# State-space layer of a 12-layer kernel: the bounds of plus and minus ten on B times delta, on GpSimd instead of VectorE

## Chip, cores and metric

The kernel runs on one core of a Trainium2 chip, as one launch that computes all twelve layers. The metric is the device time of that launch in microseconds (us), lower is better. Each engine has its own in-order queue of instructions: TensorE (PE in the profile, its weight loads PEld), VectorE (DVE), ScalarE (ACT), GpSimd (POOL) and SyncE (SP), which only issues DMAs. Engines are ordered against each other by semaphores alone.

## What is computed

The input is x of 64 sequences of 32 tokens with 128 features, so 2048 tokens. Twelve layers follow one another, each `x = x + layer(layernorm(x))`. The change touches the second one, the state-space layer `_L0_attn_ref`, whose front part is this (S is 16 states per feature):

```python
delta = jax.nn.softplus(x @ W_delta + b_delta)
Bm, Cm = x @ W_B, x @ W_C
A = -jnp.exp(A_log)
def step(h, inp):
    x_t, d_t, B_t, C_t = inp
    bar_A = jnp.exp(jnp.minimum(d_t[..., None] * A, 10.0))
    bar_B = jnp.clip(d_t[..., None] * B_t[:, None, :], -10.0, 10.0)
    h = jnp.clip(bar_A * h + bar_B * x_t[..., None], -10000.0, 10000.0)
    y_t = jnp.sum(h * C_t[:, None, :], axis=-1) + x_t * D_param
    return h, y_t
```

Behind it every token goes through the two best of four gated experts (a router, SiLU of one product times another, a root mean square norm, a down projection), and the sum is normed again.

## The kernel before, in words

The class `L0Attn` keeps features on the 128 partitions and tokens along the free axis. The 2048 tokens are cut into four quarters of 512 tokens (16 sequences of 32). For each quarter there are 16 states, so the layer has 64 units of work that the code calls states j = 0 to 63, each a tile of 128 x 512 fp32 words. All tiles lie in one SBUF tensor, `arena`; `PS` is PSUM. The tile `Ur[j % 8]` is used in place through a state's whole life, a ring of eight:

- TensorE (line 1002) spreads row B of the state over the partitions into PSUM; VectorE multiplies it by delta into `Ur` (line 1324, event `a0_db`).
- VectorE bounds it to plus and minus ten with one two-operation `tensor_scalar` in place (line 1334, `a0_clipped`).
- GpSimd multiplies it by x in place (line 1189, `a0_u`).
- ScalarE made the decay `Ar` (line 1122, an exponential); VectorE runs the recurrence over the tokens with `tensor_tensor_scan` on `Ar` and `Ur` (line 1329, `a0_scanned`).
- TensorE spreads row C (line 1002 again); VectorE multiplies (line 1319, `a0_read`); TensorE adds the result into PSUM with an identity matrix (line 1046). After 16 states VectorE adds x times D (line 1313) and the quarter is done.

All engines walk the same numbered steps i, in program order, and the order of the work is written out by hand as offsets from i. In step i VectorE does, in this order: the product with C of state i-3, the product with B of state i, the scan of state i-2, the bounds of state i, and then whatever else is due. GpSimd in step i does the product with x of state i-1. The quarters are staggered: what the next quarter needs first is made within the steps of the one before (`prepare`, three steps of each quarter with VectorE work in them, lines 1225 to 1236: steps 3, 5, 8, 19, 21, 24, 35, 37 and 40), the finished quarter's y at steps 20, 36 and 52, its routing (lines 1259 to 1303) above all at steps 24, 40 and 56.

From step 22 on, one expert of one quarter (a unit) is worked off in every four steps: TensorE's matmuls (lines 1013, 1021, 1032), ScalarE's SiLU, squares and scaling (lines 1150, 1157, 1164), on VectorE two products in two of the four steps (line 1348) and two tiny instructions (lines 1355 and 1362), on GpSimd a root (`root_pool`, line 317, a power of a 128 x 4 tile) at offset 8 and an addition of a 128 x 512 tile (line 1200) at offset 10. In GpSimd's order both stand behind the product with x of their step. The last scan's steps are 64 and 65; from then to the end only experts are left, and after the sixteenth unit the next layer follows.

Four more lines are compared below: on GpSimd the copies of lines 3038 and 3039 and the clearing of line 1808, and the pair of lines 1937 and 1940, of which the second waits on the same engine for the first. All lie in other layers.

Of the kernel before, what the change touches and what calls it, by code (L numbers as in the profile page):

```python
# [10 lines left out]
ALU = mybir.AluOpType  # L11
# [173 lines left out]
def quarter(ap, q):  # L185
    return ap[:, 4 * q:4 * q + 4, :]
# [10 lines left out]
def cut(q):  # L197
    return slice(QW * q, QW * q + QW)
# [111 lines left out]
def root_pool(e, T, g, x, tag, event):  # L310

    half = g.C["minus_half"][0:x.shape[0]]
    for ax in range(2, len(x.shape)):
        half = half.unsqueeze(ax)
    for w in T.due(event):
        e.wait_ge(*w)
    e.tensor_tensor(x, x, half.broadcast_to(list(x.shape)), ALU.pow).then_inc(*T.done("norm_root", tag))  # L317
# [598 lines left out]
class L0Attn(Layer):  # L916
# [259 lines left out]
    def pool(self, e, T):  # L1176
        g, SN, E = self.g, self.SN, self.E
        self.start_pool(e, T)
        for w in T.due(("in_weights", "first")):
            e.wait_ge(*w)  # L1180
        e.tensor_copy(self.select, g.C["select"]).then_inc(*T.done("a0_select", 0))
        e.memset(self.Ar.rearrange("p r (b t) -> p (r b) t", t=S)[:, :, 0:1], 0.0).then_inc(*T.done("a0_zero", 0))
        for i in range(self.STEPS):
            j = i - 1
            if 0 <= j < self.STATES:
                u = self.Ur[:, j % self.RING, :]
                for w in T.due(("a0_clipped", j)):
                    e.wait_ge(*w)
                e.tensor_tensor(u, u, g.XT[:, self.part(j)], ALU.mult).then_inc(*T.done("a0_u", j))  # L1189
            n = self.unit(i, 8)  # L1190
            if n is not None:
                at = 4 * self.place(n)[0]
                root_pool(e, T, g, self.ms[:, at:at + 4], ("a0", n), ("a0_ms", n))
            n = self.unit(i, 10)
            if n is not None:
                q = self.place(n)[0]
                a = quarter(self.acc, q)
                for w in T.due(("a0_scaled", n), ("a0_acc", q), ("a0_summed_out", n - 1)):
                    e.wait_ge(*w)
                e.tensor_tensor(a, a, self.tmp[n % 2], ALU.add).then_inc(*T.done("a0_summed_out", n))  # L1200
            q = self.last(i, 12)
            if q is not None:
                root_pool(e, T, g, self.total[:, 4 * q:4 * q + 4], ("a0_total", q), ("a0_totals", q))
            q = self.last(i, 13)
            if q is not None:
                x = quarter(g.X, q)
                for w in T.due(("a0_normal", q)):
                    e.wait_ge(*w)
                e.tensor_tensor(x, x, quarter(self.acc, q), ALU.add).then_inc(*T.done("a0_added", q))
            if i in self.ROOT_AT:  # L1210
                self.follower.begin_pool(e, T, self.ROOT_AT[i])

    def dve(self, e, T):
# [94 lines left out]
        for i in range(self.STEPS):  # L1308
            q = self.ended(i, 20)
            if q is not None:  # L1310
                for w in T.due(("a0_summed", SN * q + SN - 1)):
                    e.wait_ge(*w)
                e.scalar_tensor_tensor(out=self.yT[:, cut(q)], in0=g.XT[:, cut(q)], scalar=W["a0_D"], in1=PS[:, self.YB, :],
                                       op0=ALU.mult, op1=ALU.add).then_inc(*T.done("a0_y", q))
            j = i - 3
            if 0 <= j < self.STATES:
                for w in T.due(("a0_c", j), ("a0_scanned", j)):
                    e.wait_ge(*w)
                e.tensor_tensor(self.Ur[:, j % R, :], PS[:, self.CB, :], self.Ur[:, j % R, :], ALU.mult).then_inc(*T.done("a0_read", j))
            u = self.Ur[:, i % R, :]  # L1320
            if i < self.STATES:
                for w in T.due(("a0_b", i), ("a0_delta", i // SN), ("a0_summed", i - R)):
                    e.wait_ge(*w)
                e.tensor_tensor(u, PS[:, self.BB, :], delta[:, self.part(i)], ALU.mult).then_inc(*T.done("a0_db", i))
            j = i - 2
            if 0 <= j < self.STATES:
                for w in T.due(("a0_decay", j), ("a0_u", j)):
                    e.wait_ge(*w)
                e.tensor_tensor_scan(self.Ur[:, j % R, :], self.Ar[:, j % R, :], self.Ur[:, j % R, :], 0.0, ALU.mult,  # L1329
                                     ALU.add).then_inc(*T.done("a0_scanned", j))  # L1330
            if i < self.STATES:
                for w in T.due(("a0_db", i)):
                    e.wait_ge(*w)
                e.tensor_scalar(u, u, -10.0, 10.0, ALU.max, ALU.min).then_inc(*T.done("a0_clipped", i))  # L1334
            q, k = self.prep(i)
            if q is not None:
                prepare(q, k)
            for k in range(2):
                q = self.ended(i, 23 + k)
                if q is not None:  # L1340
                    route(q, k)
            for f in range(2):
                n = self.unit(i, 2 + f)
                if n is not None:
                    k = n % 2
                    for w in T.due(("a0_silu", (n, f)), ("a0_up", (n, f)), ("a0_down", n - 2), ("a0_square", (n - 2, f))):
                        e.wait_ge(*w)
                    e.tensor_tensor(self.gT[k][:, f, :], PS[:, self.UB + f, :], self.sg[k][:, f, :],
                                    ALU.mult).then_inc(*T.done("a0_gated", (n, f)))
            n = self.unit(i, 7)  # L1350
            if n is not None:
                ms = self.ms[:, 4 * self.place(n)[0]:4 * self.place(n)[0] + 4]
                for w in T.due(("a0_meansq", n), ("a0_weight", n - 1)):
                    e.wait_ge(*w)
                e.tensor_scalar(ms, PS[:, self.MB, 0:4], 1.0 / F, 1e-6, ALU.mult, ALU.add).then_inc(*T.done("a0_ms", n))
            n = self.unit(i, 8)
            if n is not None:
                q, x = self.place(n)
                rows = slice(4 * q, 4 * q + 4)
                for w in T.due(("norm_root", ("a0", n)), ("a0_scaled", n - 1)):  # L1360
                    e.wait_ge(*w)
                e.tensor_tensor(self.gate[:, rows], self.ms[:, rows], self.probs[:, rows, x], ALU.mult).then_inc(*T.done("a0_weight", n))
            q = self.last(i, 12)
            if q is not None:
                total = self.total[:, 4 * q:4 * q + 4]
                for w in T.due(("a0_outsq", q)):
                    e.wait_ge(*w)
                e.tensor_scalar(total, total, 1.0 / D, 1e-6, ALU.mult, ALU.add).then_inc(*T.done("a0_totals", q))
            if i in self.STATS_AT:
                self.follower.begin_dve(e, T, self.STATS_AT[i], ("a0_added", self.STATS_AT[i]))  # L1370
            if i in self.ROWS_AT:
                self.follower.begin_rows_dve(e, T, self.ROWS_AT[i])
            q = self.last(i, 13)
            if q is not None:
                for w in T.due(("norm_root", ("a0_total", q))):
                    e.wait_ge(*w)
                for t in range(4 * q, 4 * q + 4):
                    m = e.scalar_tensor_tensor(out=self.acc[:, t, :], in0=self.acc[:, t, :], scalar=self.total[:, t:t + 1],
                                               in1=W["a0_normw"], op0=ALU.mult, op1=ALU.mult)
                m.then_inc(*T.done("a0_normal", q))  # L1380
# [2953 lines left out]
```

## Time and profile before

| | |
|---|---|
| three runs | 2205.10, 2211.74, 2214.41 us, median 2211.74 |
| span of the profiled execution, first to last instruction | 2208.0 us |
| busy: PE, DVE, ACT, POOL | 1833.8, 1512.9, 976.1, 729.9 us |
| steps of the 64 states | from 118 to 345 us |

The time that the profiled execution itself took is not given apart; its span lies among the three times. The clock of TensorE is given as a share of 2.4 GHz. In the timeline a row has the start and the duration in us, the engine, the line, the operation, the tile written and the tile read with their shapes, and in brackets how long the engine had been idle before it and what released it. The start that is recorded is the one at which the instruction begins on its engine; rows of one engine may overlap by some hundredths.

### The profile page before, as it was taken

What the parts mean: (1) busy time and instruction counts of PE and PEld (TensorE: products, weight loads), DVE (VectorE), ACT (ScalarE), POOL (GpSimd) and SP (SyncE); (2) the same over time, 40 slices, a digit from 0 to 9 for tenths busy, and PEclk for the clock granted to TensorE, in tenths of its full rate; (3) what the DMA queues carried; (4) which work ended last, traced back from release to release, by engine and by line L of the source; (5) the groups of instructions that cost most, each with busy time, mean ns of one, the idle gap of its engine ahead of it and who ended that gap; (6) DMA issues with size and microseconds to landing.
All of it is one profiled execution on the core that took longest, in us unless ns stands there. A gap on an engine that the chain in (4) does not pass through costs nothing. (4 is left out here: it accounts for less than half of the span.)

```text
span 2208.0 us, 49959 instructions
## 1 busy us (share of the span) xinstructions
PE 1833.8 (83%) x20130; PEld 1190.9 (54%) x20130; DVE 1512.9 (69%) x3632; ACT 976.1 (44%) x2471; POOL 729.9 (33%) x951
## 2 busy tenths in 40 slices
PE   6768999899878789986677699999999987757596
PEld 2313556555545556643557466666666652225386
DVE  4799995688875665557861577666766569987732
ACT  3455754566643722242412355555555421115243
POOL 1333554455540524214340501000000046633443
PEclk9878999999999999998779999999999998876698
DMA  9100000100016100070034101000000000021087
GB/s 352 61 1 1 1 1 1 73 4 5 5 77 260 55 2 1 3 322 2 2 118 145 45 20 39 11 20 20 20 11 10 1 1 10 19 91 77 30 289 239
DMA packets 56085, 134.78 MB, mean 61 GB/s; under 512 B 13913, under 2 KB 34092, under 8 KB 48176
## 3 DMA queue, kind: packets, MB, share of 16 engines
q1 hardware_dynamic: 52560, 125.48, 15.9%
q0 software_dynamic: 3296, 6.12, 0.8%
q8 instruction: 159, 2.61, 0.5%
q14 instruction: 70, 0.57, 0.1%
HBM read 112.13 MB, written 20.12 MB: 60 GB/s over the span
## 5 line engine op out<-in xcount | busy, mean ns | idle before, releaser
L317 POOL TENSOR_TENSOR arena<-arena 128x4 f32<-128x4 f32 (+2 forms) x97 | 113.9, 1175 | 816.1 <-DVE arena L261 358.9
L3223 ACT ACTIVATE arena<-PS,arena 128x289 f32<-128x289 f32 x256 | 127.0, 506 | 177.3 <-DVE arena L3328 177.2
L1803 POOL TENSOR_TENSOR arena<-arena 128x128 f32<-128x128 f32 x384 | 140.8, 405 | 44.3 <-PE PS L1666 20.8
L3111 PE MATMUL PS<-arena 128*128 128x289 f32 x512 | 136.2, 409 | 2.3 <-DVE arena L3322 1.8
L1739 DVE RECIPROCAL arena<-PS 128x128 f32<-128x128 f32 x96 | 91.6, 955 | 51.4 <-PE PS L1704 51.2
L1770 ACT COPY arena<-PS 32x128 f32<-32x128 f32 x384 | 99.5, 259 | 51.3 <-PE PS L1680 46.7
L364 PE MATMUL PS<-arena 128*128 128x512 f32 x208 | 110.7, 657 | 12.5 <-DVEq L4134 11.7
L1189 POOL TENSOR_TENSOR arena<-arena 128x512 f32<-128x512 f32 x64 | 84.0, 1313 | 109.6 <-DVE arena L1334 109.6
L3111 PEld LDWEIGHTS PS<-arena 128*128 128x128 f32 x512 | 92.8, 192 | 24.5 <-issue 2.6
L3328 DVE TENSOR_REDUCE arena<-PS 128x2 f32<-128x578 f32 x128 | 92.5, 753 | 7.3 <-PE PS L3111 6.1
L2448 PE MATMUL PS<-arena 128*128 128x512 f32 x192 | 90.9, 608 | 0.0
L456 PE MATMUL PS<-arena 128*128 128x128 f32 (+4 forms) x576 | 81.6, 286 | 11.2 <-DVE arena L411 4.1
L384 PE MATMUL PS<-arena 128*128 128x128 f32 x288 | 50.4, 316 | 47.8 <-DVE arena L288 17.7
L1785 ACT ACTIVATE arena<-arena 128x512 f32<-128x512 f32 x96 | 60.5, 631 | 64.1 <-DVE arena L1732 62.0
L456 PEld LDWEIGHTS PS<-arena 128*128 128x128 f32 (+1 forms) x576 | 75.5, 206 | 24.2 <-issue 7.1
L420 PE MATMUL PS<-arena 128*128 128x512 f32 x160 | 81.8, 631 | 7.4 <-DVE arena L411 3.8
L3125 PE MATMUL PS<-arena 128*128 128x128 f32 x512 | 77.6, 281 | 11.7 <-DVE arena L3341 10.8
L3341 DVE TENSOR_SCALAR arena<-arena 128x290 f32<-128x290 f32 x256 | 83.9, 371 | 4.6
L1329 DVE TENSOR_TENSOR_SCAN arena<-arena 128x512 f32<-128x512 f32 x64 | 86.3, 1348 | 0.0
L403 ACT COPY arena<-PS 128x512 f32<-128x512 f32 x40 | 24.4, 609 | 133.6 <-PE PS L384 133.5
L1666 PE MATMUL PS<-arena 32*32 32x128 f32 x3072 | 55.8, 299 | 32.9 <-DVE arena L1732 22.1
L3101 PE MATMUL PS<-arena 128*128 128x128 f32 x512 | 69.9, 286 | 13.9 <-ACT arena L3240 7.1
(412 smaller groups left out, 4746.0 us busy)
## 6 DMA issues: line engine op xcount, KB each, us to landing
arena<-in_ctx SPq DMA_DIRECT2D x48, 1090.0 KB, 8.9
arena<-in_f_w SPq DMA_DIRECT2D x39, 514.0 KB, 5.6
lists<-arena SPq DMA_DIRECT2D x8, 1040.0 KB, 9.9
arena<-in_f_w SPq DMA_DIRECT2D x32, 256.0 KB, 2.9
arena<-in_ctx SPq DMA_DIRECT2D x16, 512.0 KB, 3.7
arena<-in_mid SPq DMA_DIRECT2D x1, 3796.5 KB, 11.7
arena<-in_late SPq DMA_DIRECT2D x1, 3204.0 KB, 10.3
arena<-in_w SPq DMA_DIRECT2D x1, 3017.0 KB, 13.1
```

The source lines that it names most:

```text
L317: e.tensor_tensor(x, x, half.broadcast_to(list(x.shape)), ALU.pow).then_inc(*T.done("norm_root", tag))
L364: e.matmul(g.PS[:, b, :], g.C["ident"], g.const_words[:, 0:512], start=True, stop=True)
L456: i = e.matmul(g.PS[:, b, n * j:n * j + n], src[:, at:at + P], w_, start=True, stop=True)
L1189: e.tensor_tensor(u, u, g.XT[:, self.part(j)], ALU.mult).then_inc(*T.done("a0_u", j))
L1329: e.tensor_tensor_scan(self.Ur[:, j % R, :], self.Ar[:, j % R, :], self.Ur[:, j % R, :], 0.0, ALU.mult, ALU.add).then_inc(*T.done("a0_scan ...
L1739: e.reciprocal(rest, PS[:, 7, P:2 * P]).then_inc(*T.step())
L1770: k = e.copy(v[r, :, h, :], PS[r, 4, 0:P].rearrange("p (a d) -> p a d", d=HD))
L1803: k = e.tensor_tensor(dst[:, b], spread(src[:, b, :], [P, HG, S], 1), spread(self.g.C["headmask"], [P, HG, S], 2), ALU.mult)
L2448: e.matmul(g.PS[:, b, :], w_, g.XT[:, cut(q)], start=True, stop=True).then_inc(*T.done(name, k))
L3111: m = e.matmul(PS[:, k, 0:UL], self.qt[i % 2][:, j, P * k:P * k + P], self.kt[i % 3][:, j, :], start=True, stop=True)
L3223: e.activation(self.weights(n, k, 0, UL), PS[:, k, 0:UL], ACT.Exp, bias=self.st[:, h, k:k + 1], accum_out=self.st[:, h, 4 + k:5 + k]).then ...
L3328: e.tensor_reduce(self.st[:, n % 2, 2 * k:2 * k + 2], PS[:, 2 * k:2 * k + 2, 0:UL], AXX, ALU.max, negate=True).then_inc(*T.done("k3_least" ...
```

## The change

The bounds leave VectorE's queue, where they stood behind the scan, and go into GpSimd's, in front of the product with x of the same state. GpSimd now waits for `a0_db` of state j, bounds, waits for its own `a0_clipped`, and multiplies.

```diff
@@ pool()
             j = i - 1
             if 0 <= j < self.STATES:
                 u = self.Ur[:, j % self.RING, :]
+                for w in T.due(("a0_db", j)):
+                    e.wait_ge(*w)
+                e.tensor_scalar(u, u, -10.0, 10.0, ALU.max, ALU.min).then_inc(*T.done("a0_clipped", j))
                 for w in T.due(("a0_clipped", j)):
                     e.wait_ge(*w)
                 e.tensor_tensor(u, u, g.XT[:, self.part(j)], ALU.mult).then_inc(*T.done("a0_u", j))
@@ dve()
                 e.tensor_tensor_scan(self.Ur[:, j % R, :], self.Ar[:, j % R, :], self.Ur[:, j % R, :], 0.0, ALU.mult,
                                      ALU.add).then_inc(*T.done("a0_scanned", j))
-            if i < self.STATES:
-                for w in T.due(("a0_db", i)):
-                    e.wait_ge(*w)
-                e.tensor_scalar(u, u, -10.0, 10.0, ALU.max, ALU.min).then_inc(*T.done("a0_clipped", i))
             q, k = self.prep(i)
             if q is not None:
                 prepare(q, k)
```

## Rows read from the trace of the kernel before

**Rows 1.** Busy time by stretch: us from start, each engine's busy time (instructions), clock, DMA

```profile
118.00:170.00 52.00, 39.27 (x75) 11.56 (x74) 51.66 (x75) 21.55 (x33) 23.93 (x19) 0.76 0.00 1
170.00:222.00 52.00, 42.81 (x141) 20.98 (x141) 48.74 (x83) 28.00 (x42) 20.59 (x17) 0.87 0.00 1
222.00:275.00 53.00, 49.56 (x214) 30.12 (x214) 51.50 (x94) 38.95 (x69) 26.02 (x22) 0.94 0.00 1
275.00:345.00 70.00, 63.80 (x272) 36.38 (x271) 69.55 (x117) 37.69 (x72) 39.79 (x32) 0.94 0.00 1
```

**Rows 2.** Waits of VectorE, 118 to 345 us: total, times, longest

```profile
DVE arena L1319 <- PE PS L1002: 3.5, 3, 1.4
```

**Rows 3.** Waits of TensorE, 275 to 345 us

```profile
PE PS L1002 <- DVE arena L1319: 3.5, 4, 1.2
```

**Rows 4.** Groups by line, 118 to 345 us: count, busy and mean, idle before, releaser

```profile
L1329 DVE TENSOR_TENSOR_SCAN arena<-arena 128x512 f32<-128x512 f32 x64 | 86.3, 1348 | 0.0
L1334 DVE TENSOR_SCALAR arena<-arena 128x512 f32<-128x512 f32 x63 | 28.3, 449 | 0.0
...
L1189 POOL TENSOR_TENSOR arena<-arena 128x512 f32<-128x512 f32 x64 | 84.0, 1313 | 109.6 <-DVE arena L1334 109.6
L1200 POOL TENSOR_TENSOR arena<-arena 128x512 f32<-128x512 f32 x9 | 13.5, 1501 | 6.7 <-ACT arena L1164 6.7
L317 POOL TENSOR_TENSOR arena<-arena 128x4 f32<-128x4 f32 x12 | 12.2, 1016 | 5.7 <-DVE arena L1355 3.2 <-DVE arena L1368 2.4
```

**Rows 5.** Timeline of VectorE, a step without expert work

```profile
152.36 0.40 DVE L1334 TENSOR_SCALAR arena<-arena 128x512 f32<-128x512 f32 x1
152.67 0.68 DVE L1319 TENSOR_TENSOR arena<-PS,arena 128x512 f32<-128x512 f32 x1
153.27 0.67 DVE L1324 TENSOR_TENSOR arena<-PS,arena 128x512 f32<-128x512 f32 x1
153.87 1.31 DVE L1329 TENSOR_TENSOR_SCAN arena<-arena 128x512 f32<-128x512 f32 x1
155.10 0.39 DVE L1334 TENSOR_SCALAR arena<-arena 128x512 f32<-128x512 f32 x1
```

**Rows 6.** Timeline of GpSimd over the same step

```profile
152.83 1.27 POOL L1189 TENSOR_TENSOR arena<-arena 128x512 f32<-128x512 f32 x1 [1.48 <-DVE arena L1334]
155.58 1.27 POOL L1189 TENSOR_TENSOR arena<-arena 128x512 f32<-128x512 f32 x1 [1.48 <-DVE arena L1334]
```

**Rows 7.** Timeline of VectorE around 281 us

```profile
280.35 1.30 DVE L1329 TENSOR_TENSOR_SCAN arena<-arena 128x512 f32<-128x512 f32 x1
281.57 1.42 DVE L1334 TENSOR_SCALAR arena<-arena 128x512 f32<-128x512 f32 x1
```

**Rows 8.** Timeline of GpSimd around 281 us

```profile
279.30 1.26 POOL L1209 TENSOR_TENSOR arena<-arena 128x512 f32<-128x512 f32 x1 [2.52 <-DVE arena L1378]
280.53 2.18 POOL L1189 TENSOR_TENSOR arena<-arena 128x512 f32<-128x512 f32 x1
282.67 1.45 POOL L1200 TENSOR_TENSOR arena<-arena 128x512 f32<-128x512 f32 x1
```

**Rows 9.** Timeline of VectorE: the same scan's place in two units

```profile
288.54 1.21 DVE L1329 TENSOR_TENSOR_SCAN arena<-arena 128x512 f32<-128x512 f32 x1
...
301.83 1.21 DVE L1329 TENSOR_TENSOR_SCAN arena<-arena 128x512 f32<-128x512 f32 x1
```

**Rows 10.** Lines of GpSimd elsewhere: least, median and longest duration in ns

```profile
L3038 POOL COPY arena<-arena x32: 228/239/486, 1247.3 to 1688.3; 128x64 f32<-128x64 f32 x32
...
L3039 POOL COPY arena<-arena x32: 178/188/189, 1247.8 to 1688.5; 128x2 f32<-128x2 f32 x32
...
L1808 POOL MEMSET arena<- x9: 519/527/665, 401.4 to 1976.8; 128x512 f32 x9
```

**Rows 11.** Timeline of GpSimd: an instruction that waits for the one before it

```profile
441.47 1.05 POOL L1937 TENSOR_TENSOR arena<-arena 128x512 f32<-128x512 f32 x1 [7.31 <-DVE arena L1994]
442.60 1.09 POOL L1940 TENSOR_TENSOR arena<-arena 128x512 f32<-128x512 f32 x1
```

## The prediction

> **What bounds the kernel now.** I read the times first, then the page, then the busy time by stretch, because a share over 2208 us says nothing of 64 steps that take about a tenth of it. In the stretches from 118 to 345 us [rows 1] the reader is to see VectorE busy for 51.66 of 52, 48.74 of 52, 51.50 of 53 and 69.55 of 70 us, while GpSimd is at less than 60% throughout. TensorE climbs from 39 of 52 us to 64 of 70 as the experts come in. The waits say the same: VectorE waits for TensorE's rows of C for 3.5 us in all [rows 2], and GpSimd sits idle for 109.6 us waiting for the bounds [rows 4]. So VectorE's queue sets the pace, and taking 64 instructions out of it looks like a plain gain. The page's chain of waits does not reach back to this layer, so it neither supports nor denies this. TensorE has little room itself: from 275 to 345 us its wait for VectorE's product is 3.5 us [rows 3].
>
> Then the single step. Without expert work it takes 155.10 - 152.36 = 2.74 us [rows 5]: bounds 0.31 (start to next start), product with C 0.60, with B 0.60, scan 1.23. GpSimd's multiplication lies at 152.83 to 154.10 [rows 6] and laps 0.23 us over the scan that starts at 153.87; that scan takes 1.31 us where free ones take 1.21 [rows 9]. At 281 us the same is seen large. The scan issued at 280.35 ends at 281.65, 1.09 after GpSimd's addition ends at 280.56; GpSimd's multiplication, issued at 280.53, takes 2.18 us and ends at 282.71, 1.06 after the scan; VectorE's bounds, issued at 281.57, take 1.42 and end at 282.99, 0.28 after the multiplication; GpSimd's next addition, issued at 282.67, ends at 284.12, 1.13 after the bounds [rows 7, 8]. Scan, bounds and GpSimd's tensor work exclude each other, and the one that asked first goes first. VectorE's products that read PSUM run beside GpSimd undisturbed (0.68 and 0.67 us under a multiplication [rows 5, 6]).
>
> This is the real bound for the change: work is not moved from a full engine to an idle one, but from a 0.31 us hold of a shared thing to a longer hold of the same thing.
>
> The Trainium skill names it (SBUF — State Buffer, "Who interferes with whom"): GpSimd's only pair of ports is VectorE's second one, and a VectorE instruction with two SBUF inputs fully blocks against a GpSimd one that reads SBUF. On rows 7 and 8 the trace agrees. By that rule the moved bounds, which read SBUF, exclude the scan too; no row here has a one-input GpSimd instruction against a scan.
>
> **The change part by part.**
>
> *Removed:* 64 instructions of VectorE. The mean is 0.449 us [rows 4], some of it waiting; 0.31 us is what one takes of the queue [rows 5], 64 x 0.31 = 20 us. That is the ceiling of what the removal itself can give.
>
> *Added:* 64 two-operation bounds on GpSimd, 128 x 512 in place. No row shows one; call its free duration c. From below: clearing the same shape takes 0.527 us [rows 10]. Next up: the copies cost 0.188 us for 2 elements and 0.239 for 64, 0.82 ns for each further element, so a copy of 512 is an estimated 0.61 us. From above: the multiplication with two inputs and one operation, 1.27 us [rows 6]. I take 0.75: one input like the copy, plus two operations that a copy has not. The ends 0.53 and 1.27 are kept. The Trainium skill (GPSIMD Engine Reference, "Elementwise — side-by-side cycle accounting") gives 1.03 cycles an element for bodies of one or two operations, an estimated 0.56 us with the small copies' overhead; by it the sum below would be some 5 to 10 us lower.
>
> *The new wait within GpSimd*, from bounds to multiplication: the pair in another layer has its second start 0.08 us after the first's end [rows 11], so 0.08.
>
> *Where the new instruction starts.* It waits for the product with B. VectorE issues the scan directly behind that product, before GpSimd can see the semaphore. So in every step the scan asks first and the bounds stand behind it. From the end of one multiplication to the next the chain is: scan 1.08, bounds c - 0.21 (the blocked multiplication of rows 8 ended 1.06 behind the scan instead of 1.27), wait 0.08, multiplication 1.27: together c + 2.22. VectorE's products, 1.20 us, fit beside GpSimd's c + 1.14. Nothing waits for the multiplication's result itself: its scan comes two steps later.
>
> *Steps 0 to 21.* Sixteen have only the basic work: from 2.74 to c + 2.22 = 2.97, +0.23 each, +3.7 us. Six carry a preparation or the quarter's y (0.6 us or more beside the lock); there about 0.3 each is won, -2 us.
>
> *Steps 22 to 63*, ten and a half units. A unit takes 301.83 - 288.54 = 13.29 us now [rows 9]. Afterwards the shared thing is held for 4 x (c + 2.22) + 1.06 for the blocked addition = 12.94 us: -0.35 each, -3.7 us. GpSimd's root (1.016 us [rows 4]) stands behind the multiplication of its step. If it runs under the scan, it costs almost nothing, else up to 0.9; I take 0.25 a unit, +2.6 us.
>
> *DMAs and other queues:* none moved. ScalarE's decays, TensorE's matmuls and SyncE's queue keep their work; the ring of eight tiles is not stretched, since the scan's place is unchanged.
>
> *Sum at c = 0.75:* 3.7 - 2 - 3.7 + 2.6 = +0.6, about +1 us. *At c = 1.27:* 16 x 0.75 = 12, the six others +1, units 4 x 3.49 + 1.06 - 13.29 = +1.73 or 18 us, root 2.6, less some 8 us that the three routing steps and the four other laden ones absorb: about +25. *At c = 0.53:* 0, -3, and units at -1.23, -13, with roots +2: -14 if TensorE could follow. From 222 to 345 us TensorE has 123 - 113.4 = 9.6 us unbusy [rows 1], so I stop at -9.
>
> The sum stands against the profiled execution, 2208.0 us of span; the three runs have their median 3.7 us above that span, and I put the forecast on the median: 2211.7 + 1 = 2213 us.
>
> **The rivals.** What a measurement of this kernel can tell from no change is about 0.5%, 11 us.
>
> *A, the forecast:* the lock carries the steps, c between 0.6 and 1.0, -6 to +10 us. It is borne out by the closed chain of blocked instructions in rows 7 and 8. Chance 0.56.
>
> *B, slower: GpSimd's bounds cost like its multiplication or more.* The place is GpSimd between the product with B and the multiplication; price c = 1.27, +25 us, 2237. It decides from c = 1.03 on: each 0.1 us of c costs about 4 to 6 us over 64 steps, so 11 us are passed there. For it: GpSimd's tensor instructions are expensive for their shape, and two operations may be two passes. Against it: the copy's 0.82 ns an element. Within B I count another order of the port: if GpSimd, going straight from multiplication to bounds, kept the thing twice in a row, VectorE would then stand still and have both products uncovered, up to 1.2 us in two steps. The scan at 280.35 went ahead of the waiting GpSimd instruction, which speaks against that. Chance 0.31.
>
> *C, faster: a one-input instruction on GpSimd does not hold the scan up, or is cheap.* Then the step is VectorE's alone, 2.74 - 0.31 = 2.43 us; 20 us would be won, of which TensorE's room of 9.6 us in the experts' steps, and some 5 in the first ones, let 11 to 16 through: 2198. Against it: both VectorE's one-input bounds and its scan are seen blocked by GpSimd. Chance 0.13. By the Trainium skill's rule above it does not happen by the port.
>
> *D, the change does nothing:* not likely as such, since VectorE's queue is full; it would look like A.
>
> **How the numbers follow.** Faster by over 0.5% is C, 0.13; within 0.5% is A, 0.56; slower is B, 0.31. The likeliest is A with 2213. For 8 in 10, the lower end takes in A's bottom and about half of C: 2201. The upper end takes in c = 1.27 with a little for the order of the port: 2240.
>
> **What would show each step.** Right: line 1334's group gone from VectorE, a one-input group on GpSimd with a mean of c plus about 0.9 us of waiting behind scans, scans at a mean above 1.35 us because most begin under a multiplication, a plain step near 2.97, GpSimd no longer idle waiting for VectorE for long. VectorE's busy time will hardly fall, since blocked scans count as busy. Wrong: scans at 1.21 throughout (then C), a plain step at 3.4 or more (then B), or GpSimd's bounds that start and end under a scan. If TensorE's waits for VectorE in 275 to 345 us vanish and VectorE shows waits for line 1002 in their place, TensorE took the gain.

## The result, and the profile after

The kernel after takes 2243.93 us (median of four runs, 2238.53 to 2246.27), the kernel before 2213.07 (four runs): ratio 1.0154, 95% interval 1.0132 to 1.0175, so 31 us by the medians and 34 by the ratio. The forecast was no change, 2213; 2243.9 lies above the upper end of its range, 2240. An execution now and then is far slower than the others of its kernel, and the ratios leave such ones out, here two of the eleven of w128 (6890.63 and 3887.44 us).

The busy time by stretch of the kernel after, columns as in [rows 1], with one stretch more because the steps last longer:

```profile
118.00:170.00 52.00, 42.29 (x64) 11.72 (x62) 46.80 (x50) 19.70 (x29) 49.40 (x32) 0.57 0.00 0
170.00:222.00 52.00, 42.62 (x123) 18.82 (x124) 47.91 (x66) 26.60 (x37) 47.70 (x29) 0.82 0.00 1
222.00:275.00 53.00, 42.97 (x180) 25.66 (x179) 44.06 (x68) 32.09 (x52) 49.03 (x31) 0.94 0.00 0
275.00:345.00 70.00, 55.23 (x226) 30.58 (x225) 54.21 (x81) 32.44 (x62) 65.08 (x42) 0.93 0.00 1
345.00:381.00 36.00, 30.30 (x123) 17.98 (x122) 26.71 (x39) 15.37 (x33) 32.75 (x21) 0.91 0.00 1
```

VectorE was full in [rows 1]; now it has 4 to 16 us free in every stretch, and GpSimd, the fifth engine column, is busy for 91 to 95% of each. The bound has changed engine. The groups by line, 110 to 385 us, beside [rows 4]:

```profile
L1189 POOL TENSOR_SCALAR arena<-arena 128x512 f32<-128x512 f32 x64 | 134.0, 2094 | 20.7 <-DVE arena L1327 15.6
L1192 POOL TENSOR_TENSOR arena<-arena 128x512 f32<-128x512 f32 x64 | 87.1, 1361 | 5.3
L317 POOL TENSOR_TENSOR arena<-arena 128x4 f32<-128x4 f32 x12 | 12.3, 1026 | 2.5 <-DVE arena L1354 1.8 <-DVE arena L1367 0.7
...
L1332 DVE TENSOR_TENSOR_SCAN arena<-arena 128x512 f32<-128x512 f32 x64 | 100.1, 1564 | 16.5 <-POOL arena L1192 15.7 <-ACT arena L1122 0.7
```

The bounds (line 1189 now) take 2.09 us on GpSimd where they took 0.45 on VectorE, GpSimd's idle time of 109.6 us before the product has become 20.7 + 5.3, and the scan, which had waited for nobody, waits 15.7 us for GpSimd's product. One plain step shows the order, first VectorE, then GpSimd, beside [rows 5, 6]:

```profile
153.01 0.68 DVE L1327 TENSOR_TENSOR arena<-PS,arena 128x512 f32<-128x512 f32 x1
153.98 1.67 DVE L1332 TENSOR_TENSOR_SCAN arena<-arena 128x512 f32<-128x512 f32 x1 [0.29 <-POOL arena L1192]
155.75 0.69 DVE L1322 TENSOR_TENSOR arena<-PS,arena 128x512 f32<-128x512 f32 x1
...
157.33 1.67 DVE L1332 TENSOR_TENSOR_SCAN arena<-arena 128x512 f32<-128x512 f32 x1 [0.29 <-POOL arena L1192]
```

```profile
152.61 1.27 POOL L1192 TENSOR_TENSOR arena<-arena 128x512 f32<-128x512 f32 x1
153.96 1.91 POOL L1189 TENSOR_SCALAR arena<-arena 128x512 f32<-128x512 f32 x1
155.96 1.27 POOL L1192 TENSOR_TENSOR arena<-arena 128x512 f32<-128x512 f32 x1
157.31 1.91 POOL L1189 TENSOR_SCALAR arena<-arena 128x512 f32<-128x512 f32 x1
```

A step is 157.33 - 153.98 = 3.35 us instead of 2.74, and it is GpSimd's: bounds 1.91, a wait 0.09, product 1.27, a wait 0.08. VectorE stands 0.29 us until the product is done, which then lets both go on: the bounds of the next state 0.08 us and the scan 0.10 us after it. The scan begins 0.02 us behind the bounds, takes 1.67 instead of 1.21 us and ends while the bounds are still running. Two of VectorE's waits, 110 to 385 us, say who is late:

```profile
DVE arena L1361 <- POOL arena L317: 22.9, 10, 2.6
DVE arena L1332 <- POOL arena L1192: 15.7, 23, 2.0
```

In the experts' steps a unit, read as [rows 9] from one root of GpSimd to the same place in the next unit, is 292.03 - 275.38 = 16.65 us instead of 13.29:

```profile
275.38 1.02 POOL L317 TENSOR_TENSOR arena<-arena 128x4 f32<-128x4 f32 x1
...
292.03 1.03 POOL L317 TENSOR_TENSOR arena<-arena 128x4 f32<-128x4 f32 x1
```

For all that follows I use one length from each trace: from the start of the first scan to the end of the last. Before it is 120.24 to 344.26, 224.0 us; after 119.64 to 380.05, 260.4 us, +36.4. Of this the span shows 32.7 (2240.7 against 2208.0): before, TensorE ran behind VectorE at the end of the steps, and y of the last quarter was only added 6.7 us after the last scan (350.94 us), after it is 3.3 us (383.35). The first 20 intervals between scans, those with no expert product yet, grew from 61.5 to 69.5 us, +8.0; the other +28.4 lie in the steps with experts. The length itself is not exact: in micro, below, whose steps are those of the kernel before, it is 227.2, with the first part again 61.5, so a difference of some 3 us in it says nothing. Chips differ: the kernel before had medians of 2213, 2223 and 2225 us on the three that were used, so every ratio is against the kernel before on the same chip.

### The profile page after: what moved, and what is told of

Same layout as the page of the kernel before. It is cut to its first block and busy times, and to the rows that moved or that the text cites. A ratio compares the mean times of both kernels' runs of the same rounds, so it can differ in the third digit from the quotient of the medians.

```text
span 2240.7 us, 49959 instructions
## 1 busy us (share of the span) xinstructions
PE 1857.5 (83%) x20130; PEld 1198.4 (53%) x20130; DVE 1510.1 (67%) x3568; ACT 976.3 (44%) x2471; POOL 864.4 (39%) x1015
## 5 line engine op out<-in xcount | busy, mean ns | idle before, releaser
L1189 POOL TENSOR_SCALAR arena<-arena 128x512 f32<-128x512 f32 x64 | 134.0, 2094 | 20.7 <-DVE arena L1327 15.6
L364 PE MATMUL PS<-arena 128*128 128x512 f32 x208 | 117.0, 690 | 12.7 <-DVEq L4133 11.9
L1332 DVE TENSOR_TENSOR_SCAN arena<-arena 128x512 f32<-128x512 f32 x64 | 100.1, 1564 | 16.5 <-POOL arena L1192 15.7
L1002 PE MATMUL PS<-arena 96*128 96x512 bf16 x128 | 53.5, 459 | 48.0 <-DVE arena L1322 36.8
L2447 PE MATMUL PS<-arena 128*128 128x512 f32 x192 | 90.7, 607 | 0.0
L420 PE MATMUL PS<-arena 128*128 128x512 f32 x160 | 82.7, 636 | 7.9 <-DVE arena L411 4.1
L1192 POOL TENSOR_TENSOR arena<-arena 128x512 f32<-128x512 f32 x64 | 87.1, 1361 | 5.3
L3124 PE MATMUL PS<-arena 128*128 128x128 f32 x512 | 77.4, 280 | 11.4 <-DVE arena L3340 10.9
L384 PE MATMUL PS<-arena 128*128 128x128 f32 x288 | 49.0, 310 | 43.8 <-DVE arena L288 16.0
L1046 PE MATMUL PS<-arena 128*128 128x512 f32 x128 | 82.3, 731 | 2.1 <-DVE arena L1316 2.1
```

The lines of the kernel that those rows point to most:

```text
L364: e.matmul(g.PS[:, b, :], g.C["ident"], g.const_words[:, 0:512], start=True, stop=True)
L3124: m = e.transpose(PS[:, b, P * k:P * k + P], self.weights(n, k, at, at + P), g.C["ident"])
```

## The experiments

**Theory Q**: GpSimd's two-operation bounds are slow by themselves, and its in-order queue carries the steps. **Rival P**: the port that GpSimd shares with VectorE's scans makes them long. **Rivals L and R**: not the duration costs, but the order or the extra wait (L), or the root that comes late (R).

**micro: the price by itself.**

```diff
 # kernel before, pool(), ahead of the state loop; w is a loaded weight tile
+e.tensor_scalar(self.sg[0][:, 0, :], w[:, 0:512], -10.0, 10.0, ALU.max, ALU.min)
+e.tensor_scalar(self.sg[0][:, 1, 0:256], w[:, 0:256], -10.0, 10.0, ALU.max, ALU.min)
+e.tensor_scalar(self.sg[1][:, 0, 0:128], w[:, 0:128], -10.0, 10.0, ALU.max, ALU.min)
+e.tensor_scalar(self.sg[1][:, 1, :], w[:, 0:512], -10.0, None, ALU.max)
+e.tensor_tensor(self.sq[0][:, 0, :], w[:, 0:512], w[:, 512:1024], ALU.mult)
+e.tensor_copy(self.sq[1][:, 0, :], w[:, 0:512])
```

> The kernel before, with six extra GpSimd instructions on scratch tiles in front of the state loop, where GpSimd is idle: two-operation bounds over 512, 256 and 128 columns, a one-operation bound over 512, a product of two tiles over 512, a copy over 512. Theory Q (GpSimd's two-operation bounds are slow by themselves, whatever VectorE does): 512 columns take 1.9 us here too, and the time grows in proportion to the columns (about 1.0 and 0.57 for 256 and 128); the one-operation bound takes about half to two thirds. Rival P (the 1.91 us are mostly waiting for a shared port behind the scan): alone they take 0.6 to 0.9 us. Kernel time within 2 us of the kernel before.

The timeline of GpSimd:

```profile
105.08 1.94 POOL L1184 TENSOR_SCALAR arena<-arena 128x512 f32<-128x512 f32 x1
107.08 1.06 POOL L1185 TENSOR_SCALAR arena<-arena 128x256 f32<-128x256 f32 x1
108.20 0.63 POOL L1186 TENSOR_SCALAR arena<-arena 128x128 f32<-128x128 f32 x1
108.90 1.49 POOL L1187 TENSOR_SCALAR arena<-arena 128x512 f32<-128x512 f32 x1
110.45 1.26 POOL L1188 TENSOR_TENSOR arena<-arena 128x512 f32<-128x512 f32 x1
111.66 0.60 POOL L1189 COPY arena<-arena 128x512 f32<-128x512 f32 x1
```

Outside the steps the bounds take 1.94 us too, and the time follows the columns: (1.94 - 0.63) / 384 = 3.4 ns each, and 0.19 fixed. Rival P, waiting for the port, is out as the reason for the 1.91. The copy is at 0.60, the prediction's estimate for it was 0.61; what it did not foresee is that the first operation adds 0.89 us to a copy and the second 0.45. The kernel took 2209.99 us in its one run.

**none: the ceiling.**

```diff
 # kernel after, pool(); a0_u now waits for a0_db
-e.tensor_scalar(u, u, -10.0, 10.0, ALU.max, ALU.min).then_inc(*T.done("a0_clipped", j))
```

> The bounds are left out altogether (that part of the layer is not computed). This is the ceiling of taking them from VectorE. The prediction's arithmetic: a plain step at 2.43 us instead of 2.74, VectorE's queue 20 us shorter, of which TensorE lets 11 to 16 through: 2197 to 2202 us. If GpSimd's product and the scan really exclude each other in full, a plain step is 1.08 + 1.27 or a little more, about 2.4, the same. If TensorE bounds the steps with experts harder than thought, only 5 us are gained.

Measured 2193.99 us, ratio 0.9925 (0.9907 to 0.9943), 13 to 21 us faster; length of the steps 209.6 us, -14.4, of which -5.1 in the first 20 intervals and -9.3 behind them. A plain step is 2.52 us, not 2.43. VectorE, then GpSimd:

```profile
153.63 1.22 DVE L1329 TENSOR_TENSOR_SCAN arena<-arena 128x512 f32<-128x512 f32 x1
154.95 0.69 DVE L1319 TENSOR_TENSOR arena<-PS,arena 128x512 f32<-128x512 f32 x1
```

```profile
153.79 2.11 POOL L1189 TENSOR_TENSOR arena<-arena 128x512 f32<-128x512 f32 x1 [0.41 <-DVE arena L1324]
```

The product with C must wait for the scan just in front of it (0.10 us of idle that the bounds used to cover), and GpSimd's product, which now asks just behind the scan, takes 2.11 us, of which 0.84 are waiting for it. So the bounds were worth 17 us (by the ratio) to 19 (by the medians) on VectorE, near the 20 of the prediction; its 11 to 16 let through hold the 14.4 of the steps and overlap the interval of 13 to 21.

**half: every other state.**

```diff
 # pool(): bounds only if j % 2 == 1; dve(), behind the scan: bounds only if j % 2 == 0
```

> Odd states are bounded on GpSimd, even ones on VectorE. Theory Q (GpSimd's queue became the bound, 1.91 + 1.27 us and two waits a step): over two steps GpSimd needs 1.91 + 2 x 1.27 + 0.25 = 4.7 us, less than VectorE's 5.2, so most of the loss vanishes: before -5 to +8 us (2208 to 2221). Rival P (every moved bound costs its share through the port): half of the 31 us, +15 (2228). Rival L (a scan gets its input too late, which the ring and the step distance decide): any value, with VectorE waiting for GpSimd's product in front of the scans behind odd states.

Measured ratio 1.0121 (1.0102 to 1.0141), length 258.8 us, +34.8. This is a miss of theory Q in its plain form: half the work on GpSimd, nearly the full loss. It is a miss of rival P's half share too (+15; the ratio gives +23 to +31). Two plain steps take 6.30 us. VectorE, then GpSimd:

```profile
157.03 1.31 DVE L1333 TENSOR_TENSOR_SCAN arena<-arena 128x512 f32<-128x512 f32 x1
...
159.65 1.22 DVE L1333 TENSOR_TENSOR_SCAN arena<-arena 128x512 f32<-128x512 f32 x1
160.78 1.43 DVE L1339 TENSOR_SCALAR arena<-arena 128x512 f32<-128x512 f32 x1
```

```profile
155.99 1.27 POOL L1193 TENSOR_TENSOR arena<-arena 128x512 f32<-128x512 f32 x1 [0.36 <-DVE arena L1339]
157.35 2.71 POOL L1190 TENSOR_SCALAR arena<-arena 128x512 f32<-128x512 f32 x1
160.13 1.79 POOL L1193 TENSOR_TENSOR arena<-arena 128x512 f32<-128x512 f32 x1
```

Read as a loop: GpSimd's product ends at 157.26, the waiting scan runs to 158.34, the bounds behind it end at 160.06, 1.72 later; GpSimd's next product is queued behind the next scan (ends 160.87) and ends at 161.92; VectorE's bounds, issued at 160.78, wait for it and take 1.43 us; and GpSimd's product for that even state waits for those bounds (0.36 us idle). GpSimd's own work is not the limit (1.91 and twice 1.27 in 6.30 us), the port passes from one to the other. So besides its duration, a tensor instruction on GpSimd costs what it makes others queue.

**w128, w256, w128b: the duration alone.** Order, count and waits are those of the change.

```diff
 # kernel after, pool(); 128 columns in w128 and w128b, 256 in w256
-e.tensor_scalar(u, u, -10.0, 10.0, ALU.max, ALU.min)
+e.tensor_scalar(u[:, 0:128], u[:, 0:128], -10.0, 10.0, ALU.max, ALU.min)
```

> The kernel after, with GpSimd's bounds over the first 128 of 512 columns only (the other three quarters stay unbounded). Order, waits and count are those of the change; only the duration c falls, to an estimated 0.55 us. Theory Q with the prediction's sum c + 2.22: a plain step at 2.77, total before -9 to 0 us (2204 to 2213). Rival L or P (order, waits, or the port at each instruction are what costs): at least +10 us stays (2223 or more).

Measured ratio 0.9978 (0.9965 to 0.9991), 4 to 5 us faster. Nothing of the loss stays, so the order and the added wait make no loss without the duration. They are not shown to be free: of the 17 to 19 us that none gained, 12 to 15 are missing here, and this run does not divide them between order, wait and the 0.63 us. The profile was taken from a second run of the same kernel:

> The kernel after with GpSimd's bounds over 128 of 512 columns (the rest stays unbounded), once more, for its profile. Alone these bounds take 0.63 us. By the prediction's chain c + 2.22 a plain step is 2.85 us, with every bounds instruction queued behind a scan (duration 0.63 + 0.9 = 1.5 us) and VectorE never waiting for GpSimd's product. If the chain is wrong, the plain step is VectorE's alone (2.5 us) or the bounds run beside the scan.

One time of 2221.85 us beside a median before of 2222.94; length 224.9, +0.9. A plain step, GpSimd then VectorE:

```profile
152.72 1.43 POOL L1189 TENSOR_SCALAR arena<-arena 128x128 f32<-128x128 f32 x1
...
155.58 1.42 POOL L1189 TENSOR_SCALAR arena<-arena 128x128 f32<-128x128 f32 x1
```

```profile
152.16 1.55 DVE L1332 TENSOR_TENSOR_SCAN arena<-arena 128x512 f32<-128x512 f32 x1
...
155.03 1.55 DVE L1332 TENSOR_TENSOR_SCAN arena<-arena 128x512 f32<-128x512 f32 x1
```

The step is 2.86 us, by the prediction's chain 0.63 + 2.22 = 2.85; the bounds take 1.43, so 0.80 of it waiting behind the scan.

> The kernel after with GpSimd's bounds over 256 of 512 columns (half stays unbounded), c = 1.06 us alone. Theory Q (GpSimd's queue alone: c + 1.27 + 0.17 per step) gives 2.50 us, less than VectorE's step, so nothing lost: 2194 to 2208 us. The prediction's port chain (c + 2.22 = 3.28 per plain step, since the bounds start behind the scan) gives +8 to +20 us: 2221 to 2233.

Measured ratio 1.0062 (1.0037 to 1.0087), +8 to +19 us; length 241.9, +17.9. Plain theory Q asked for no loss and is refuted for this width; the chain gives 1.06 + 2.22 = 3.28, and the trace shows 3.28 from one scan to the next:

```profile
152.14 1.97 DVE L1332 TENSOR_TENSOR_SCAN arena<-arena 128x512 f32<-128x512 f32 x1
...
155.42 1.98 DVE L1332 TENSOR_TENSOR_SCAN arena<-arena 128x512 f32<-128x512 f32 x1
```

**one: one operation, all columns.**

```diff
-e.tensor_scalar(u, u, -10.0, 10.0, ALU.max, ALU.min)
+e.tensor_scalar(u, u, 10.0, None, ALU.min)
```

> The kernel after with one operation in GpSimd's instruction (only the upper bound; the lower one is left out), c = 1.49 us alone. Theory Q: 1.49 + 1.27 + 0.17 = 2.93 us a plain step, total +5 to +15 (2218 to 2228). Port chain c + 2.22 = 3.71 us: more than the two-operation form in the kernel after (3.35), +30 us or more (2243 and up), because the shorter bounds let GpSimd catch up and then always start behind the scan.

Measured ratio 1.0051 (1.003 to 1.0071), +7 to +16 us; length 242.8, +18.8. Here theory Q has it, and the chain's 3.71 fails: plain steps at 2.92, Q's sum was 2.93. GpSimd, then VectorE:

```profile
154.07 1.49 POOL L1189 TENSOR_SCALAR arena<-arena 128x512 f32<-128x512 f32 x1
155.64 1.27 POOL L1192 TENSOR_TENSOR arena<-arena 128x512 f32<-128x512 f32 x1
```

```profile
154.15 1.61 DVE L1332 TENSOR_TENSOR_SCAN arena<-arena 128x512 f32<-128x512 f32 x1
```

An instruction with c = 1.49 gives a shorter plain step than one with 1.06, although the two kernels are equal as a whole (242.8 and 241.9). There are two orders of the port. In the first (w128, w256) the scan asks first, GpSimd's bounds wait, and the step is c + 2.22. In the second (one, after) the scan asks some hundredths of a us after the bounds, and the step is GpSimd's queue, c + 1.44: 2.93 and 3.35. The second is possible because the bounds let the scan in early. It ends 1.69 us behind the bounds' start in both kernels (155.76 - 154.07; 155.65 - 153.96); as a waiting scan ends 1.08 after its release [rows 5, 6], the bounds free the port after some 0.6 us, whether they then run to 1.49 or 1.91. A scan of the kernel after that asks only 0.60 us behind the bounds' start shows the same directly: it takes 1.21 us, as a free one, with the bounds running all the while.

```profile
317.47 1.91 POOL L1189 TENSOR_SCALAR arena<-arena 128x512 f32<-128x512 f32 x1
```

```profile
318.07 1.21 DVE L1332 TENSOR_TENSOR_SCAN arena<-arena 128x512 f32<-128x512 f32 x1
```

**reorder: the bounds on VectorE, and the port in another order.**

```diff
 # kernel before, dve(), step i
-product with C of i-3; product with B of i; scan of i-2; bounds of i
+product with B of i; product with C of i-3; bounds of i; scan of i-2
```

> The kernel before (bounds on VectorE) with another order within VectorE's step: product with B of state i, product with C of state i-3, bounds of i, scan of i-2. If the port between GpSimd's product and the scan costs what the trace shows, the product now asks while the scan holds it, ends 1.06 us after the scan and so inside the 1.2 us of the two PSUM products of the next step: a plain step at 2.65 instead of 2.74, scans at 1.21, no bounds at 1.4: -4 to -12 us (2201 to 2209). If the gain is lost to TensorE, which sees the product with C later, or if the port is no cost, within 2 us of the kernel before.

Measured ratio 1.003 (1.0011 to 1.0048): slower, a miss. The plain step is 2.65 as expected (the scan starts at 153.62 and again at 156.26), all 64 scans together fell from 86.3 to 80.3 us, yet the length grew to 229.6. In the experts' steps something else is now queued behind GpSimd. VectorE, then GpSimd:

```profile
263.61 1.17 DVE L1362 TENSOR_TENSOR arena<-arena 128x4 f32<-128x4 f32 x1
...
268.55 1.48 DVE L1328 TENSOR_SCALAR arena<-arena 128x512 f32<-128x512 f32 x1
```

```profile
262.64 2.12 POOL L1189 TENSOR_TENSOR arena<-arena 128x512 f32<-128x512 f32 x1 [0.80 <-DVE arena L1328]
```

A product of four columns with both inputs in SBUF, 0.15 us otherwise, takes 1.17 and ends at 264.78, 0.02 behind GpSimd's product (264.76); the bounds take 1.48 behind GpSimd's addition. Seven of the nine such products within the steps are long: 8.4 us together instead of 1.4, and the 63 bounds 31.5 instead of 28.3. What the scans no longer wait (6.0 us), others do. That this is the whole loss is argued, not shown: the length grew by 5.6 us and is good to some 3.

**half_re: the half kernel in that order.**

```diff
 # half, dve(), step i: the order of reorder
```

> Odd states bounded on GpSimd, even ones on VectorE, as before in this study, but VectorE's step in the order product with B, product with C, bounds, scan. The loop seen in the half kernel (6.30 us for two plain steps) hung on VectorE's bounds queued behind GpSimd's product, which was queued behind the scan. If that chain of port waits is the cause of its loss, the new order breaks it: two plain steps at 5.3 to 5.6 us, total within 10 us of the kernel before (ratio 0.995 to 1.005). If the loss belongs to each moved bounds, it stays near 1.012.

Ratio 1.0034 (1.0015 to 1.0053), length 235.6, +11.5 instead of +34.8. Two thirds of half's loss are gone with the same 32 bounds on GpSimd, so that part belongs to the order in which the port is asked for. The groups name the largest piece: 31 of the bounds left on VectorE took 37.4 us in half, 1.21 each, queued behind GpSimd as in the loop above, and take 17.9 here, 0.58 each, 19.5 of the 23.2 us by which the length fell. But the plain pair is 6.02 us (2.38 and 3.64), not the 5.3 to 5.6 expected; the gain came in the experts' steps.

**add_dve and root_first: GpSimd's other work in the kernel after.**

```diff
 # add_dve: the experts' addition, pool() to the end of dve()'s step
-[pool] e.tensor_tensor(a, a, self.tmp[n % 2], ALU.add).then_inc(*T.done("a0_summed_out", n))
+[dve]  e.tensor_tensor(a, a, self.tmp[n % 2], ALU.add).then_inc(*T.done("a0_summed_out", n))
 # root_first: in pool()'s step
-bounds; product with x; root
+bounds; root; product with x
```

> The kernel after, with the experts' addition into the accumulator (one a unit of four steps) taken from GpSimd and put at the end of VectorE's step. Theory Q (GpSimd's in-order queue carries every step: bounds 1.91, product 1.27, two waits, and a unit's root and addition on top, 16.65 us a unit): a unit loses 1.2 to 2.2 us, 10 units: 12 to 20 us off the kernel after (2224 to 2232 if the kernel before is at 2213; ratio to before 1.006 to 1.010). Rival (port conflicts between scan and GpSimd carry it, wherever the tensor instruction stands): within 4 us of the kernel after (ratio 1.014 or more), since the addition on VectorE reads two SBUF tiles and competes as before.

Ratio 1.0145 (1.01 to 1.0189): the value lies in the rival's band (1.014 or more), but the interval is too wide to tell the theories apart. The trace says more: length 252.9, 7.5 us shorter than after. Taking 1.27 us a unit from GpSimd did shorten the steps, by about half of the 12 to 20 that Q asked for, so neither theory fits as it stood.

> The kernel after, with the experts' root ahead of the product with x in GpSimd's step (behind the bounds) instead of behind it. GpSimd's total work is the same. Theory Q: VectorE's wait for the root (22.9 us in ten places) is cover, not cost, since GpSimd has no idle time anyway: within 5 us of the kernel after (ratio 1.013 to 1.017). Rival R (VectorE standing in line for the root is what makes a unit longer than the sum of GpSimd's work): 8 to 12 us off (ratio 1.010 to 1.012).

Ratio 1.0169 (1.0128 to 1.021), length 260.4, to 0.1 us that of the kernel after. VectorE's waits, 110 to 390 us:

```profile
DVE arena L1336 <- POOL arena L1196: 14.2, 21, 2.0
DVE arena L1365 <- POOL arena L317: 13.0, 11, 1.4
```

Its wait for the root fell from 22.9 to 13.0 us and bought nothing. Rival R falls: those waits are VectorE's idle time beside a full GpSimd.

## Why the prediction was wrong, point by point

**The term that failed is c**, the free duration of the two-operation bounds on GpSimd, taken as 0.75 us with ends of 0.53 and 1.27. It is 1.91 in the steps and 1.94 alone (micro), outside both ends. The copy was a sound row for what it was (0.61 estimated, 0.60 measured), but the upper end was taken from a product with two inputs as though a second input were dearer than an operation with constants. In rival B stood that "two operations may be two passes", and it was not priced: twice a copy would have given no more than 1.2 either. The Trainium skill's rule (GPSIMD Engine Reference, "Elementwise — side-by-side cycle accounting": 1.03 cycles an element for one or two operations) was further off still. The 0.56 us that the prediction took from it does not come out: at that section's 1.2 GHz it is 0.44 us, with the copies' 0.19 an estimated 0.63. Micro's 3.4 ns an element, against 0.86 by the rule, contradicts it for this instruction.

**The chain c + 2.22 was right for short bounds.** It gives 2.85 and 3.28 for c = 0.63 and 1.06, and w128b and w256 show 2.86 and 3.28. The threshold, "from c = 1.03 on" slower by over 0.5%, is not refuted and not shown: w256 at 1.06 came out at 0.62% with an interval from 0.37, and one at 1.49 at 0.51% (from 0.30 to 0.71). At c = 0.75 the kernel would probably have been about where I put it: w128 with 0.63 is 0.2% faster, w256 with 1.06 is 0.6% slower.

**The chain does not reach 1.91.** It would give 4.13 a step; the kernel has 3.35, because "in every step the scan asks first and the bounds stand behind it" turns around and because the bounds hold the port for 0.6 us of their time, not for all of it. Rival B had the turned order in its text, GpSimd "going straight from multiplication to bounds" and VectorE standing still, and spoke against it; the rows of after show it, with 0.29 us of standing a step. The Trainium skill has the lock held for the full instruction (SBUF — State Buffer, "SBUF: two separate sides"); rows 7 and 8 and the 2.11 us of none agree for products, the bounds of after and one do not. By the chain the loss at 1.91 would have been some 16 x 1.39 + 10.5 x 4.29 = 67 us before covers, about twice what was measured.

**Named right, weighed too low.** The mechanism of the loss is rival B's (GpSimd between the product with B and the multiplication, at 0.31), with its price of 25 us measured as 31 to 34. That the two are close is luck: the price was for c = 1.27 and a step of 3.49, and 1.91 with a port that is freed early gives 3.35, two errors that offset each other. "VectorE's busy time will hardly fall": 1512.9 to 1510.1 us. Scans "at a mean above 1.35 us": 1.56. The sign "a plain step at 3.4 or more (then B)": 3.35, just short of it. "Nothing waits for the multiplication's result itself": wrong, 23 scans did.

**Rival C** had TensorE let 11 to 16 us of 20 through, some 5 in the first steps and 9.6 with the experts. None's steps gave 5.1 in the first 20 intervals and 9.3 behind them. The numbers are near, the reason is not shown: the 9.6 were read from 222 us on, while the experts begin about 182, and TensorE still had 12.9 us unbusy from 174 to 327 us of none, against 14.2 from 182 to 345 before, with a granted clock of 0.98 instead of 0.92 over these stretches. And VectorE's nine products of four columns took 8.5 us in none's steps instead of 1.4, as in reorder, so the port kept a part of the 20.

**Left open:** how the 36.4 us (8.0 before the experts, 28.4 with them) split between GpSimd's own time and the port in the experts' steps. From after's groups, 134.0 - 64 x 1.91 = 11.8 us of the bounds and 87.1 - 64 x 1.27 = 6 of the products are waiting, but how much of that lies on the path was not separated; add_dve recovered 7.5.

## What to carry to other kernels

Price an instruction on an engine from a row of the same operation there, and if there is none, let the range go well past the nearest kind: a copy and a product did not bracket an elementwise instruction with two constants. Before work is moved to the idle one of two engines that share a port, add up what each step holds of it and see who asks first; here half the dose cost nearly all of the loss, and another order gave two thirds of that back. A waiting time that a change creates on an engine that has become idle is no cost by itself: root_first halved one and gained nothing.

## What was not expected of the hardware

- On GpSimd a two-operation `tensor_scalar` of 128 x 512 fp32 takes 1.94 us, with one operation 1.49, a copy 0.60, a product of two tiles 1.26. On VectorE the same two-operation instruction takes 0.40 [rows 5].
- With 512 columns such an instruction frees the shared port by 0.6 us after its start: a scan that asks 0.02 us behind the two-operation form ends 0.2 us before it does, one that asks 0.60 us behind takes 1.21 us. A product holds the port to its end (a scan ends 1.08 us behind that).
- A VectorE product of 128 x 4 with both inputs in SBUF took 1.17 us instead of 0.15 behind a GpSimd product (reorder).
